# Unread matmuls in two gaps of TensorE: in the first chunk of the linear attention and in double steps 1 and 2 of the softmax attention

## The chip, the cores and the metric

One core of one Trainium2 chip runs the whole kernel. The metric is the device time of one launch in microseconds (us). TensorE (PE) multiplies matrices into the eight banks of PSUM; VectorE (DVE), ScalarE (ACT) and GpSimd (POOL) work on what it leaves there; SyncE (SP) starts transfers. The engines run at the same time, each in its own order, and wait for one another through semaphores. The profile also gives the clock that TensorE was granted in each stretch: 1.00 is 2.4 GHz, 0.50 is 1.2 GHz.

## The reference

A small language model tower on two sequences of 2048 tokens and 128 features: token embedding plus position, then a linear-looking attention with 8 heads of 16, then a block with a softmax attention of 2 heads of 64 and a dense mixture of 8 experts of width 512.

```python
h = tok(x)                                   # embedding + position
h = h + attn(layernorm(h))                   # 8 heads: scores masked, normed, no softmax
h = h + ffn(layernorm(h))                    # 2 heads softmax attention, then 8 experts

# attn
dots = where(causal_mask, 0.0, q @ k.T * scale)
mu = diagonal(cum_mean(dots)); t = dots - mu
s = diagonal(cum_mean(t * t))
out = where(causal_mask, 0.0, t * rsqrt(s + EPS) * norm_g + norm_b) @ v

# ffn
scores = where(causal, l2norm(q) @ l2norm(k).T * sqrt(dh), min)
y = (softmax(scores) @ v) @ Wo
out = sum_e softmax(y @ gate_W + gate_b)[e] * (gelu(y @ W1[e] + b1[e]) @ W2[e] + b2[e])
```

## The kernel before

The two sequences are worked on side by side. There are three stages, and each engine has its own program, written out by hand; only semaphores order the engines against one another.

**The linear attention** goes through 16 chunks of 128 tokens of each sequence. From chunk 1 on (`step_a`) it needs only running sums of earlier chunks. Chunk 0 has no earlier chunk and is computed directly. For each sequence b, PE makes the masked scores (`dots`), DVE subtracts the mean (line 700, semaphore `attn0`), PE transposes the eight heads (line 1097, semaphore `attnT0_ps`), ACT copies them from banks 3 and 4 to memory (line 466, semaphore `attnT0_sb`) and PE multiplies each head with its values, as sixteen instructions of 128x16 (an fp32 matmul stands as two instructions in the profile, a transpose as one). Before its copy of sequence 0 ACT has eight squares to make (line 460). PE's order there is: transposes of sequence 0, the 128x16 set of sequence 0, transposes of sequence 1, the sums of sequence 1, the 128x16 set of sequence 1, then the transposes of chunk 2's normed rows (`xn_T`, line 1025) and chunk 1's `step_a`. `xn_T` of chunk 2 waits for DVE, which first takes the state of sequence 1 out of PSUM (line 655) and then norms the rows (line 647).

**The projections** of the softmax attention (`step_b`) follow by chunk. In the first five of its steps PE already issues `NWARM` = 4 matmuls of 128x512 in fp16 into bank 5 whose results nobody reads.

**The softmax attention** runs in 80 double steps (both heads). In step s PE makes the scores of step s (`scores`), row scores whose only use is a row maximum for a later block (`lone_scores` for the first blocks, one head at a time, into bank 3 or 4), and the products with the values of step s - 2 (`values`). Each lone score is reduced by DVE (line 860) and PE may overwrite its bank only after that (semaphore `sm_used`). Steps 0 and 1 also hold the last two chunks' transposes (`unit_T`), and the first lone scores of step 1 wait for the keys' low halves of chunk 14, which DVE makes (line 829). **The experts** fill the rest, from about 490 us on.

All matmuls are recorded under line 1017, the line of the helper `mm`. Bank 1 holds a chunk's queries and keys in the first stage and is free once ACT has read them (`qkT_sb`); bank 5 is free in steps 1 and 2 of the softmax attention.

Of the kernel before, what the change touches and what calls it, by code (L numbers as in the profile page):

```python
# [23 lines left out]
CH = 512  # L24
# [19 lines left out]
def tower(nc, ids, emb_rows, consts, consts16, rows, cols, w_qkv, w_out, w_sm, w_o, w_gate, w12_rows, b2, out):  # L44
    with ExitStack() as ctx:
        def sb(name, shape, dt=F32):
            return ctx.enter_context(nc.sbuf_tensor(name, shape, dt))

        def sem(name):
            return ctx.enter_context(nc.semaphore(name))  # L50


        cst = sb("cst", [P, C_END])
        c16 = sb("c16", [P, K16 * P], F16)
        row = sb("row", [P, R_END])
# [25 lines left out]
        ident = cst[:, C_ID:C_ID + P]  # L81
# [5 lines left out]
        minus16, onehot = c16[:, 0:P], c16[:, P:2 * P]  # L87
# [81 lines left out]
        ps = ctx.enter_context(nc.psum_tensor("ps", [P, 8, 512], F32))  # L169
# [10 lines left out]
        S = {name: sem(name) for name in names.split()}  # L180
# [832 lines left out]
        def _(pe):  # L1013
            t_ = nc.tensor

            def mm(o, l, r, start=True, stop=True):
                return t_.matmul(o, l, r, start=start, stop=stop, skip_group_check=True)  # L1017
# [42 lines left out]
            def sums(c, par, b, first=False, state=True):  # L1060
                pe.wait_ge(S["qkv_sb"], 2 * c + b + 1)
                if not first:
                    pe.wait_ge(S["x_sb"], 2 * c + b - 1)
                mm(ps[:, 5 + b, 0:D].rearrange("p (h e) -> p h e", e=DA), upper, kv[par][:, b, :, DA:2 * DA], stop=first)
                if not first:
                    mm(ps[:, 5 + b, 0:D], last_row, V1[1 - par][:, b], start=False)
                    pe.wait_ge(S["sg_ready"], 2 * c + b - 1)
                    mm(ps[:, 5 + b, D:D + HA * XW], qT[par][:, b], sg[:, b], start=False)
                if not state:
                    return  # L1070
                if not (first and b == 0):
                    pe.wait_ge(S["sgc_ready"], 2 * c + b)
                mm(ps[:, 7, 0:HA * XW], qk[par][:, b, D:], kv[par][:, b].rearrange("p h w -> p (h w)")
                   ).then_inc(S["state_ps"], 1)
# [17 lines left out]
            for b in range(B):  # L1092
                pe.wait_ge(S["attn0"], b + 1)
                if b:
                    pe.wait_ge(S["attnT0_sb"], b)
                for h in range(HA):
                    last = t_.transpose(ps[:, 3 + h // 4, h % 4 * P:(h % 4 + 1) * P], dtm[:, b, h], ident)
                last.then_inc(S["attnT0_ps"], 1)
                if b:
                    sums(0, 0, 1, first=True)  # L1100
                pe.wait_ge(S["attnT0_sb"], b + 1)
                for h in range(HA):
                    at = D + h * XW + DA
                    last = mm(ps[:, 5 + b, at:at + DA], dtm[:, b, h], kv[0][:, b, h, DA:2 * DA], start=False)
                last.then_inc(S["x_ps"], 1)
# [70 lines left out]
            def unit_T(c):  # L1176
                pe.wait_ge(S["qkn_ready"], c + 1)
                if c >= 2:
                    pe.wait_ge(S["lo_ready"], c - 1)
                if c == NT - 1:  # L1180
                    pe.wait_ge(S["vlo_ready"], NT)
                for i in range(4):
                    b = i % 2
                    last = t_.transpose(ps[:, t_bank(c), i * P:(i + 1) * P],
                                        qkn[:, b, i // 2 * P:(i // 2 + 1) * P], ident)
                last.then_inc(S["qkd_ps"], 1)
# [62 lines left out]
            def lone_scores(it, r, kb, w, k, h):  # L1249
                nonlocal guard  # L1250
                c, b = ITEMS[it]
                q, at, g = b * N + c * CH + r * P, b * N + kb * CH, k + h
                half = slice(h * DS, (h + 1) * DS)
                if g < 10:
                    pe.wait_ge(S["lo_ready"], NT - 1)
                else:
                    pe.wait_ge(S["sm_used"], g - 1)
                if it == 2 and (r, kb) == (0, 0):
                    pe.wait_ge(S["hi_ready"], NT)
                last = mm(ps[:, 3 + g % 2, 0:w], qh[half, q:q + P], kh[half, at:at + w], stop=kb < c)  # L1260
                if kb == c:
                    for z in range(2):
                        last = mask(ps[:, 3 + g % 2, w - P:w], z, h, neg_qk)
                last.then_inc(S["sm_ps"], 1)
                guard = S["sm_used"], g + 1
# [33 lines left out]
            def scores(s):  # L1299
                it, kt, r0, diag = STEPS[s]  # L1300
                c, b = ITEMS[it]
                if s == 0:
                    pe.wait_ge(S["hxT_sb"], NT)
                    pe.wait_ge(S["lo_ready"], 4)
                if s < 2:
                    pe.wait_ge(S["qkn_ready"], NT - 1)
                    pe.wait_ge(S["vlo_ready"], NT - 1)
                if s == FIRST[2]:
                    pe.wait_ge(S["lo_ready"], NT)
                if s:  # L1310
                    pe.wait_ge(S["s_used"], 2 * s - 1)
                lo, at = r0 * P, b * N + kt * P
                q0 = b * N + c * CH
                for still, moving in ((kh, qh), (kl, qh), (kh, ql)):
                    for h in range(HS):
                        half = slice(h * DS, (h + 1) * DS)
                        mm(ps[:, (2 * s + h) % 3, lo:], still[half, at:at + P], moving[half, q0 + lo:q0 + CH],
                           start=still is kh and moving is qh, stop=False)
                if diag:
                    for z in range(2):  # L1320
                        for h in range(HS):
                            mask(ps[:, (2 * s + h) % 3, lo:lo + P], z, h, neg_kq)
                if s in FIRST:
                    pe.wait_ge(S["mrow_sb"], it + 1)
                for h in range(HS):
                    half = slice(h * DS, (h + 1) * DS)
                    last = mm(ps[:, (2 * s + h) % 3, lo:], onehot[half], qm[half, it % 2, lo:], start=False)
                last.then_inc(S["s_ps"], 1)
# [54 lines left out]
            for s in range(NSTEP + LAG + 6):  # L1383
                if s < NSTEP:
                    scores(s)
                if s < 2:
                    unit_T(NT - 2 + s)
                lone = [(*part, h) for part in MSLOT.get(s, ()) if part[0] in ALONE for h in range(HS)]
                pairs = [part for part in MSLOT.get(s, ()) if part[0] not in ALONE]
                assert not (lone and pairs)  # L1390
                closing = min(len(pairs), 1) if s >= CLOSE else len(pairs) // 2
                for part in lone[:1]:
                    lone_scores(*part)
                for part in pairs[:len(pairs) - closing]:
                    pair_scores(*part)
                if s in RAT:
                    max_row(RAT[s])
                if LAG <= s < NSTEP + LAG:
                    values(s - LAG, 0)
                for part in lone[1:2]:  # L1400
                    lone_scores(*part)
                if LAG <= s < NSTEP + LAG:
                    values(s - LAG, 1)
                for part in lone[2:]:
                    lone_scores(*part)
                if s < CLOSE:
                    for part in pairs[len(pairs) - closing:]:
                        pair_scores(*part)
                for m in range(LAST):
                    if s - YAT[m] in PE_Y:  # L1410
                        out_part(m, PE_Y.index(s - YAT[m]) + 1)
                if s >= CLOSE:
                    for part in pairs[len(pairs) - closing:]:
                        pair_scores(*part)
# [82 lines left out]
NWARM = 4  # L1497
PR, QR = 6, 6
WLATE = [2, 7, 13]
LAG = 2  # L1500
CLOSE = 36
K16 = 8
PE_Y, ACT_Y, DVE_Y = [1, 2, 3, 7, 8], [1, 2, 4, 7], [3, 5, 9]
ITEMS, STEPS, FIRST, MSLOT, RAT, OAT, YAT = plan()
# [9 lines left out]
def t_bank(c):  # L1514
    return 6 if c == NT - 1 else 3 + c % 2
# [29 lines left out]
def constants():  # L1545
# [16 lines left out]
    c[:, C_POS:C_END] = pe.reshape(NT, P, D).transpose(1, 0, 2).reshape(P, NT * D)  # L1562
    c16 = np.zeros((P, K16, P), np.float16)
    c16[:, 0] = -np.eye(P)
    c16[[0, DS], 1] = 1.0
    for z in range(2):
# [3 lines left out]
        c16[:, 6 + z] = np.where(src[:, None] > i[None, :], NEG, 0.0)  # L1570
    c16 = c16.reshape(P, K16 * P)
    return c, c16
# [40 lines left out]
```

## Time and profile before

| what | value |
|---|---|
| median of 3 runs | 843.1 us (841.3 to 844.11) |
| the profiled execution, its own time | 841.75 us |
| its span, first to last instruction | 839.9 us |
| PE busy | 775.5 us, 92% of the span |
| DVE, ACT, POOL busy | 702.7, 487.1, 336.7 us |
| mean granted clock of TensorE | 0.98 |

The span is what the trace shows; 1.85 us of the execution lie outside it. An engine's busy time is summed over stages with different bounds, so a stretch is read by itself: which engine is waited for there, and at which clock TensorE ran. "PE" rows are matmuls, "PEld" rows the loads of their stationary operands.

### The profile page before, as it was taken

How to read it: one execution, taken by the hardware profiler on the slowest of the kernel's cores; microseconds unless marked ns; L12 is line 12 of the kernel's file. 1: busy time of each engine (PE TensorE's matmuls, PEld its weight loads, DVE VectorE, ACT ScalarE, POOL GpSimd, SP SyncE). 2: the span in 40 equal slices, each digit the busy share in tenths (PEclk: the TensorE clock that was granted, in tenths of full speed). 3: DMA queues.
4: the chain of work that ended last, by engine and by line, in shares of the span. 5: the costliest groups of instructions: out<-in, count | busy, mean ns of one | idle time of the engine just before them, and what ended most of it. 6: DMA issues, size and time to landing. Idle time of an engine off the chain costs nothing.

```text
span 839.9 us, 21024 instructions
## 1 busy us (share of the span) xinstructions
PE 775.5 (92%) x8208; PEld 554.4 (66%) x8208; DVE 702.7 (84%) x1575; ACT 487.1 (58%) x1023; POOL 336.7 (40%) x374
## 2 busy tenths in 40 slices
PE   1699999999888789998989989999999999999997
PEld 1578778877655455554656556777777777777775
DVE  3649989999678676777676989999999999999997
ACT  2435555555388567777888766455555555555553
POOL 6638999877575557666766621000000000000000
PEclk9879999999999899999999999999999999999999
DMA  4100111000000000000000000000000000000000
GB/s 131 57 8 20 39 38 35 17 27 14 1 1 1 26 2 2 3 2 2 2 3 2 3 13 2 5 12 8 8 5 12 5 11 5 12 4 12 2 14 13
DMA packets 9666, 12.09 MB, mean 14 GB/s; under 512 B 1856, under 2 KB 6592, under 8 KB 9568
## 3 DMA queue, kind: packets, MB, share of 16 engines
q1 hardware_dynamic: 8544, 8.65, 3.4%
q0 software_dynamic: 1024, 2.10, 0.9%
q8 instruction: 65, 1.06, 0.5%
q14 instruction: 33, 0.27, 0.1%
HBM read 8.65 MB, written 2.10 MB: 13 GB/s over the span
## 4 chain that ended last, share of the span: by engine, by line
PE 77%; DVE 11%; issue 4%; ACT 4%; POOL 3%; DMA 1%; another core or an unknown queue 0%; DVEq 0%; ACTq 0%
PE ps L1017 75%; DVE mx L865 2%; POOL ss L345 2%; DVE room L971 1%; DVE room L973 1%; ACT room L591 1%; DVE qkn L819 1%; DVE ss L804 1%; DMA h_all<-emb_rows,idx 1%; DVE och L940 1%; DVE mx L860 1%; ACT room L582 1%; PE ps L1025 1%; PE ps L1045 0%; POOL sm L282 0%
## 5 line engine op out<-in xcount | busy, mean ns | idle before, releaser
L604 ACT ACTIVATE cst<-ps,col 128x512 f32<-128x512 f32 x256 | 175.7, 688 | 161.1 <-PE ps L1017 160.3
L1017 PEld LDWEIGHTS ps<-arena,sq 128*128 128x128 f16 x3072 | 192.1, 98 | 61.8 <-DVE sq L1001 4.3
L1017 PE MATMUL ps<-arena,sq 128*128 128x128 f16 x3072 | 213.0, 219 | 0.5 <-DVE sq L1001 0.5
L1017 PE MATMUL ps<-y,arena 128*128 128x512 f16 x768 | 208.7, 382 | 1.3 <-DVE och L940 1.3
L1001 DVE TENSOR_TENSOR sq<-cst,sq 128x512 f16<-128x512 f32 x256 | 176.7, 690 | 4.4
L383 POOL TENSOR_TENSOR room<-room 128x512 f16<-128x512 f32 (+3 forms) x122 | 123.3, 1029 | 76.7 <-ACT room L591 76.0
L996 DVE CAST sq<-cst 128x512 f16<-128x512 f32 x256 | 109.2, 426 | 10.5 <-ACT cst L604 3.1
L582 ACT ACTIVATE room<-ps 128x512 f32<-128x512 f32 (+3 forms) x160 | 76.8, 534 | 45.6 <-PE ps L1017 45.3
L865 DVE TENSOR_REDUCE mx<-ps 128x2 f32<-128x1024 f32 (+2 forms) x64 | 70.2, 1096 | 35.1 <-PE ps L1017 34.9
L1017 PEld LDWEIGHTS ps<-y,arena 128*128 128x128 f16 x768 | 65.1, 98 | 34.3 <-issue 4.1
L1017 PEld LDWEIGHTS ps<-v,room 128*128 128x128 f16 x1632 | 56.1, 98 | 33.1 <-issue 14.6
L989 DVE SCALAR_TENSOR_TENSOR h_all<-ps,gs,h_all 128x128 f32<-128x128 f32 x256 | 77.1, 343 | 0.9 <-PE ps L1017 0.9
L1017 PE MATMUL ps<-v,room 128*128 128x65 f16 (+1 forms) x1632 | 66.8, 195 | 8.5 <-DVE och L940 5.1
L591 ACT CAST room<-room 128x512 f16<-128x512 f32 (+3 forms) x142 | 72.5, 562 | 0.0
L1017 PEld LDWEIGHTS ps<-room,y 128*128 128x128 f32 x512 | 64.1, 201 | 6.4 <-ACT y L466 5.4
L1017 PE MATMUL ps<-room,y 128*128 128x34 f32 (+1 forms) x512 | 63.3, 279 | 4.6 <-ACT y L466 4.6
L268 POOL TENSOR_TENSOR sm<-sm,mhalf 128x16 f32<-128x16 f32 x15 | 43.6, 2908 | 25.5 <-DVE sm L746 22.1
L1017 PE MATMUL ps<-kh,qh 64*128 64x512 f16 (+3 forms) x160 | 34.0, 363 | 12.1 <-DVE mx L865 8.6
L751 DVE TENSOR_TENSOR y<-ps,cst 128x1024 f32<-128x1024 f32 x30 | 36.3, 1210 | 7.6 <-PE ps L1017 7.6
L973 DVE TENSOR_TENSOR room<-room 128x512 f16<-128x512 f32 (+3 forms) x38 | 36.4, 957 | 3.8 <-ACT room L591 3.1
L1017 PE MATMUL ps<-y,room 64*128 64x512 f32 x128 | 36.8, 655 | 0.0
L239 POOL DMA_INDIRECT h_all<-emb_rows,idx x32 | 31.6, 988 | 10.1 <-issue 7.9
(164 smaller groups left out, 1177.1 us busy)
## 6 DMA issues: line engine op xcount, KB each, us to landing
sq<-w_rows SPq DMA_DIRECT2D x13, 256.0 KB
out<-h_all SPq DMA_DIRECT2D x32, 64.0 KB, 1.6
cst<-consts SPq DMA_DIRECT2D x1, 896.0 KB
h_all<-emb_rows,idx POOLq DMA_INDIRECT x32, 5.3
hxT<-w_rows SPq DMA_DIRECT2D x2, 256.0 KB
cst<-consts SPq DMA_DIRECT2D x1, 398.0 KB, 4.0
c<-consts SPq DMA_DIRECT2D x1, 256.0 KB, 5.5
x<-w_rows SPq DMA_DIRECT2D x1, 256.0 KB
```

The source lines that it names most:

```text
L268: g.tensor_tensor(sm[:, 4], sm[:, 3], mhalf[:].rearrange("p (b h) -> p b h", b=B), ALU.pow).then_inc(S["r_ready"], 1)
L383: g.tensor_tensor(plo[:, i % PR, lo:], p32[:, i % QR, lo:], phi[:, i % PR, lo:], ALU.subtract).then_inc(S["plo_pool"], 1)
L582: a.activation(p32[:, i % QR, lo:], ps[:, i % 3, lo:], ACT.Exp).then_inc(S["s_used"], 1)
L591: a.copy(phi[:, i % PR, lo:], p32[:, i % QR, lo:]).then_inc(S["p_ready"], 1)
L604: a.activation(hid[:, f], ps[:, HBANK[f], :], ACT.Gelu_apprx_tanh, bias=col[:, K_B1 + k:K_B1 + k + 1], scale=1.0 / WS).then_inc(S["hid_rea ...
L751: v.tensor_tensor(dtm[:, b], ps[:, 3:5, :].rearrange("p z (h j) -> p (z h) j", j=P), upper.unsqueeze(1).to_broadcast([P, HA, P]), ALU.mult ...
L865: v.tensor_reduce(mx[:, it % 2, r, kb], ps[:, 3:5, 0:w], AX, ALU.max).then_inc(S["sm_used"], 1)
L973: v.tensor_tensor(plo[:, i % PR, lo:], p32[:, i % QR, lo:], phi[:, i % PR, lo:], ALU.subtract).then_inc(S["plo_dve"], 1)
L989: v.scalar_tensor_tensor(hr, ps[:, EBANK[n % 2], r * D:(r + 1) * D], gs[:, m, r, n % E:n % E + 1], hr, ALU.mult, ALU.add).then_inc(S["eo_u ...
L996: v.tensor_copy(hhi[:, f], hid[:, f]).then_inc(S["hhi_ready"], 1)
L1001: v.tensor_tensor(hlo[:, f], hid[:, f], hhi[:, f], ALU.subtract).then_inc(S["hlo_even" if f % 2 == 0 else "hlo_odd"], 1)
L1017: return t_.matmul(o, l, r, start=start, stop=stop, skip_group_check=True)
```

## The change

It adds matmuls whose results nobody reads, at three places of PE's program, and nothing else. `ident`, `minus16` and `c16` are constants; `cst[:, 0:CH]` is the first 512 columns of the constants, in fp32, and `c16[:, 0:CH]` is fp16.

```diff
@@ the first chunk, for b in range(B) @@
                 last.then_inc(S["attnT0_ps"], 1)
                 if b:
                     sums(0, 0, 1, first=True)
+                else:
+                    pe.wait_ge(S["qkT_sb"], 2)
+                    for i in range(NWARM):
+                        mm(ps[:, 1, :], ident, cst[:, 0:CH])
                 pe.wait_ge(S["attnT0_sb"], b + 1)
@@ the softmax attention, step s @@
                     scores(s)
                 if s < 2:
                     unit_T(NT - 2 + s)
+                for i in range(WARM_C.get(s, 0)):
+                    mm(ps[:, 5, :], minus16, c16[:, 0:CH])
                 lone = [(*part, h) for part in MSLOT.get(s, ()) if part[0] in ALONE for h in range(HS)]
@@ constants of the plan @@
 CLOSE = 36
+WARM_C = {1: 5, 2: 3}
 K16 = 8
```

The orders of DVE, ACT, POOL and SP are what they were. On PE, in the first chunk, four matmuls now stand between the transposes of sequence 0 (`y` is the memory that holds its scores, `cst` the identity) and the 128x16 set of sequence 0, where before one followed the other:

```order
 L1097 MATMUL ps<-cst,y 128x128 [waits attn0]
 L1097 MATMUL ps<-cst,y 128x128 x7
+L1017 MATMUL ps<-cst 128x512 [waits qkT_sb]
+L1017 MATMUL ps<-cst 128x512 x3
 L1017 MATMUL ps<-room,y 128x16 [waits attnT0_sb]
 L1017 MATMUL ps<-room,y 128x16 x7
```

What stood there, the wait for `attnT0_sb`, now comes after the four; they wait for `qkT_sb` alone, ACT's reading of chunk 1's queries and keys.

On PE, in double step 1, five matmuls now stand between the transposes of the last chunk (`unit_T`, `qkn`) and the first lone scores (`kh,qh`, which wait for `lo_ready`):

```order
 L1017 MATMUL ps<-c 128x128 x4
 L1017 MATMUL ps<-room,c 128x384 x2
-L1184 MATMUL ps<-cst,qkn 128x128 [waits vlo_ready,lo_ready,qkn_ready]
-L1184 MATMUL ps<-cst,qkn 128x128 x3
+L1188 MATMUL ps<-cst,qkn 128x128 [waits vlo_ready,lo_ready,qkn_ready]
+L1188 MATMUL ps<-cst,qkn 128x128 x3
+L1017 MATMUL ps<-c 128x512 x5
 L1017 MATMUL ps<-kh,qh 128x128 [waits lo_ready]
 L1017 MATMUL ps<-c 128x128 x2
```

The transposes' rows stand twice only because their line number moved by four; the five matmuls are what is new, and they carry no wait.

On PE, in double step 2, three stand between the scores of step 2 (their last part is `room,c`) and the first lone score, which waits for `sm_used`:

```order
 L1017 MATMUL ps<-c 128x128 x4
 L1017 MATMUL ps<-room,c 128x256 x2
+L1017 MATMUL ps<-c 128x512 x3
 L1017 MATMUL ps<-kh,qh 128x384 [waits sm_used]
 L1017 MATMUL ps<-c 128x128 x2
```

Again nothing moved but the three.

## Rows read from the trace of the kernel before

**Rows 1.** The profile's page: span, and TensorE's granted clock in 40 slices.

```profile
span 839.9 us, 21024 instructions
...
PEclk9879999999999899999999999999999999999999
```

**Rows 2.** Stretches: from:to, length, then each engine's busy us (instructions), clock, DMA.

```profile
31.75:36.30 4.55, 0.00 (x0) 0.00 (x0) 4.28 (x9) 2.47 (x11) 1.67 (x3) 0.77 0.12 32
36.30:47.00 10.70, 10.69 (x46) 9.72 (x46) 2.10 (x10) 1.79 (x5) 5.66 (x8) 0.50 0.16 51
47.00:51.30 4.30, 4.30 (x12) 2.54 (x12) 1.23 (x1) 0.90 (x3) 0.00 (x0) 0.50 0.00 0
286.83:297.07 10.24, 9.89 (x88) 6.05 (x89) 5.40 (x10) 1.98 (x8) 2.11 (x4) 0.50 0.01 2
```

**Rows 3.** Chain of waits in the first chunk: start us, us, what.

```profile
33.20 1.96 another core or an unknown queue
...
35.25 1.02 ACT y L466
...
36.31 3.59 PE ps L1017 x16
```

**Rows 4.** The same chain in steps 2 to 4 of the softmax attention.

```profile
286.75 3.62 PE ps L1017 x36
...
291.96 5.15 PE ps L1017 x36
```

**Rows 5.** PE in order of time, first chunk: start us, us, engine, line, operation, count.

```profile
30.70 1.04 PE L1097 MATMUL ps<-cst,y 128*128 128x128 f32 x8
36.31 3.59 PE L1017 MATMUL ps<-room,y 128*128 128x16 f32 x16 [4.57 <-ACT y L466]
39.75 1.95 PE L1097 MATMUL ps<-cst,y 128*128 128x128 f32 x8
...
42.85 3.60 PE L1017 MATMUL ps<-room,y 128*128 128x16 f32 x16
...
55.08 1.87 PE L1017 MATMUL ps<-room,y 128*128 128x34 f32 x16
```

**Rows 6.** DVE in order of time, between chunk 0 and chunk 2.

```profile
43.06 0.44 DVE L655 TENSOR_TENSOR room<-ps,cst 128x272 f32<-128x272 f32 x1 [6.93 <-PE ps L1017]
...
45.74 0.60 DVE L647 TENSOR_SCALAR room<-h_all,mv,rs 128x128 f32<-128x128 f32 x2 [1.09 <-POOL rs L253]
```

**Rows 7.** PE in order of time: matmuls of the added kinds elsewhere, at clock 1.00.

```profile
238.45 1.03 PE L1017 MATMUL ps<-c 128*128 128x512 f16 x4
...
306.64 1.12 PE L1017 MATMUL ps<-room,wo 128*128 128x512 f32 x2
```

**Rows 8.** PE in order of time: gaps ahead of the lone scores of steps 1 and 2.

```profile
284.11 0.24 PE L1017 MATMUL ps<-kh,qh 64*128 64x128 f16 x2 [1.50 <-DVE kl L829]
...
286.75 0.46 PE L1017 MATMUL ps<-kh,qh 64*128 64x384 f16 x1 [0.79 <-DVE mx L860]
```

**Rows 9.** DVE in order of time: row maxima from step 2 on, with idle time before.

```profile
287.46 0.56 DVE L860 TENSOR_REDUCE mx<-ps 128x1 f32<-128x384 f32 x1 [0.43 <-PE ps L1017]
288.88 0.56 DVE L860 TENSOR_REDUCE mx<-ps 128x1 f32<-128x384 f32 x1 [0.86 <-PE ps L1017]
290.39 1.29 DVE L860 TENSOR_REDUCE mx<-ps 128x1 f32<-128x512 f32 x2 [0.96 <-PE ps L1017]
...
293.64 0.69 DVE L860 TENSOR_REDUCE mx<-ps 128x1 f32<-128x512 f32 x1 [1.10 <-PE ps L1017]
294.79 1.29 DVE L860 TENSOR_REDUCE mx<-ps 128x1 f32<-128x512 f32 x2 [0.46 <-PE ps L1017]
297.13 3.31 DVE L860 TENSOR_REDUCE mx<-ps 128x1 f32<-128x512 f32 x6 [1.06 <-PE ps L1017]
...
302.15 0.56 DVE L860 TENSOR_REDUCE mx<-ps 128x1 f32<-128x384 f32 x1 [0.21 <-PE ps L1017]
303.00 0.56 DVE L860 TENSOR_REDUCE mx<-ps 128x1 f32<-128x384 f32 x1 [0.29 <-PE ps L1017]
```

## The prediction, made before the changed kernel was run

> **What bounds the kernel now.** I read the page first. PE is busy for 92% of the span, so whatever lengthens or shortens its work in a stretch where it is the one waited for moves the end. The row of its clock [rows 1] shows it at full speed but for a few slices. A closer table of stretches [rows 2] shows two long ones at clock 0.50: from 34.25 us to 51.3 us, of which three rows stand there, and the 10.24 us from 286.83. The row from 31.75 to 36.30 has no matmul and a mean clock of 0.77: the clock fell in it, after some 2.5 us of idle PE, to 0.50. It then stayed there for 15 us, though PE was busy for 10.69 of the next 10.70. What PE did in that time was thin: sets of 128x16, transposes, sums [rows 5]. It came back only after the wide matmuls of chunk 1 (the row 47.00 to 51.30). So a busy PE isn't enough; what it does counts.
>
> The chain of waits then tells whether a slow PE matters there. In the first chunk it runs over ACT's copy and then PE [rows 3], from 36.31 on PE alone. In the softmax attention it runs over PE for 3.62 and 5.15 us of the 10.24 [rows 4]. Both stretches are on the path, and a faster PE shortens them until something else ends last.
>
> **The change, part by part.** Nothing is removed or moved; three groups of matmuls are added, and each has a price and a possible gain.
>
> *First group, price.* Four fp32 matmuls are eight instructions of 128x512. Two of that kind took 1.12 us with the tail of the second [rows 7], so eight take at most 4.5. From the end of the transposes at 31.74 (30.70 + 1.04, rows 5) they end by 36.24, and PE's next work starts at 36.31, waiting for ACT's copy. Price: nothing, as ACT's squares and copy cover it, but with hardly any room at that bound. The wait for `qkT_sb` names what ACT finished before its squares, so nothing waits.
>
> *First group, gain.* The idle time of 4.57 us [rows 5] shrinks to between 0.1 us and about 1, so I expect no fall at 34.25. What follows at full clock: the 128x16 set of sequence 0 takes 3.59 us at 0.50, and a set of sixteen 128x34 at 1.00 takes 1.87, so 1.72 less. The transposes of sequence 1 take 1.95 against 1.04, so 0.91 less. After that come more thin work and, now that PE is faster than ACT and DVE, more waiting; at half clock such work could not lift the clock in 10.7 us [rows 2], so I expect that it can't hold it either. I let the clock fall behind the transposes and leave the rest as it was: 1.72 + 0.91 = 2.6 us. Bounds: below, 0, if the thin work loses the clock at once. Above, the clock holds throughout: 10.69 + 4.30 = 15.0 us of PE work at half clock would be 7.5 at full. Of that some 1.1 goes back to a wait: from DVE's state at 43.06 to the end of its norms at 46.34 pass 3.28 us [rows 6] that PE's clock doesn't shorten. It would start at about 39.7 (half of the 6.75 us since 36.31 saved) and end at 43.0. PE would be there at about 41.9 (the second set ends at 46.40; about 4.5 us of the work before it saved). So 6.4 at most. I take 2.6, nearer to the lower end, for the thinness of what follows.
>
> The Trainium skill, "TensorE: Matmul & The Clock Gate", Part 4, says that transposes do not count as activity for the clock as matmuls do. The row of eight transposes at 39.75, at clock 0.50 from first to last, agrees, though the sets around them would explain it too. By that rule the clock falls before the transposes and the term is 1.72 instead of 2.6.
>
> *Second and third group, price.* Four fp16 matmuls of 128x512 took 1.03 us [rows 7]: about 0.26 each, the last one's tail included, so five take at most 1.3 and three 0.8. The gaps where they go are 1.50 us ahead of 284.11, ended by DVE's `kl`, and 0.79 us ahead of 286.75, ended by a row maximum [rows 8]. They fit at full clock, the three just so. If the clock were at 0.50 there they would take twice as long: about 1.1 and 0.8 us over.
>
> *Second and third group, gain.* Between 282 and 287 PE had these gaps and, between them, matmuls over half the rows of the array; the clock fell at 286.83. With both gaps filled the sparse time is gone, and I expect no fall. Then DVE's row maxima are next. In the slow stretch DVE waited for PE six times: 0.43 + 0.86 + 0.96 + 1.10 + 0.46 + 1.06 = 4.87 us [rows 9]. At full clock, later in the same loop, it still waited 0.21 and 0.29. Six waits of 0.25 leave 1.5, so the stretch shrinks by 4.87 - 1.5 = 3.4 us. Bounds: 0, if the clock falls all the same; 4.9, if no wait is left. I take 3.4, since the loop at full clock is the nearest row. From there everything, POOL and ACT too, is driven by these scores, so the gain passes on to the end.
>
> *Sum.* 2.6 + 3.4 = 6.0 us. Against the profiled execution's own time: 841.75 - 6.0 = 835.7. That execution is 1.35 us under the median, so against the median: 843.1 - 6.0 = **837.1 us**. All times below are against the median.
>
> **The rivals.**
>
> *The first gap buys nothing.* Its matmuls keep the clock for their own length, the clock falls in the thin work right behind, and it comes back with the same wide matmuls of chunk 1. For it: 10.7 us of thin work did not lift the clock [rows 2]. Against it: even a delayed fall leaves some of the first set at full clock. Time: 843.1 - 3.4 = 839.7.
>
> *The first gap buys all.* The clock holds to chunk 1: 843.1 - 6.4 - 3.4 = 833.3. For it: in other thin places the clock holds, such as the sets of 128x34 at 55.08. Against it: those stand between wide matmuls, the first chunk's don't.
>
> *The change does not do what it says in the softmax attention.* The clock falls there at another moment, for instance in the lone scores of steps 3 and 4, whose matmuls use half the rows. Then only the first term is left: 840.5. If both places fail, it is 843.1.
>
> The Trainium skill, "TensorE: Matmul & The Clock Gate", Part 1 ("What's actually happening"), says that the activity monitor runs on by itself and isn't reset when a kernel starts. No single trace can show that. By it, a fall or rise lands elsewhere from run to run, so one execution shows one draw of each place; the falls near 229 and 492 us are such draws too, and stay as they are.
>
> *Slower: the first group stands in the way.* ACT's copy started at 35.25, 2 us after its last square, and the chain puts 1.96 us of this down to an unknown releaser [rows 3]. The copy waits for the transposes' semaphore, and the transposes are drawn as ended at 31.74. If they really end at about 35.2, the eight added instructions begin there. At full clock they end 4.5 us later, at 39.7, which is 3.4 after 36.31 and eats the whole of the other gain: 843.1. At half clock they take up to 9.0 and end at 44.2, 7.9 late, less 3.4: 847.6. It makes the kernel slower from the point at which they end later than 39.7. For it: a wait that no row explains. Against it: the matmuls before and behind those transposes are drawn without a break up to 31.74, at the pitch of full clock.
>
> **How the numbers follow.** A measurement can tell about 0.3% from no change, 2.5 us here.
>
> - Forecast, 837.1 (with the first term between 1.5 and 4, the second between 2.5 and 4.5): 0.48.
> - First gap buys nothing, 839.7: 0.20; in about a quarter of this the gain stays under 2.5 us.
> - First gap buys all, 833.3: 0.10.
> - Softmax attention fails, 840.5: 0.07; about half of this under 2.5 us.
> - Both fail, 843.1: 0.08.
> - In the way: 0.07, of which 0.05 lose more than 2.5 us.
>
> Faster: 0.48 + 0.15 + 0.10 + 0.03 = 0.76. Slower: 0.05. Same: 0.19. The range goes from 834.2, which leaves out most of the case that buys all, to 840.6, which takes in the third case whole and the single failure: about 0.2 lies outside.
>
> **What the changed kernel's profile would show.** Right: eight matmuls `ps<-cst` behind the transposes at about 31.7, ended by 36.3; the 128x16 set of sequence 0 in 1.9 us instead of 3.59; no stretch at clock 0.50 between 283 and 297, and waits of DVE before its row maxima of about 0.25. Wrong: the clock back at 0.50 before 37 (first term), a 0.50 stretch of some length among the lone scores (second term), or ACT's copy, and PE's set behind it, later than 36.3, with the eight drawn ahead of it (in the way). If both stretches are at full clock and the end has not moved by about 6, another engine had taken over and the terms' cover was misread: for the second, DVE without idle time and yet no earlier.

## The result, and the profile after

The changed kernel takes 837.27 us (median, 836.6 to 837.8) where the kernel before takes 842.8 beside it: ratio 0.9942, interval 0.9922 to 0.9962, some 5 us faster. The prediction was 837.1 us. In a second series it took 837.34 against 843.66: 0.9931, interval 0.9915 to 0.9946. The profiled execution took 836.98 us, 4.8 less than the profiled one of before.

The page of the kernel after, its span and its row of the granted clock, for [rows 1]:

```profile
span 835.2 us, 21056 instructions
...
PEclk9999999999999999999999999999999999999999
```

Both dips of [rows 1] are gone at this resolution. Four stretches of after (from:to, length, busy us of PE, PEld, DVE, ACT, POOL, clock, DMA) stand against [rows 2]:

```profile
32.70:36.12 3.42, 3.42 (x12) 2.61 (x11) 3.35 (x10) 2.76 (x18) 1.04 (x2) 0.50 0.14 38
38.95:46.36 7.41, 6.00 (x49) 5.30 (x49) 2.10 (x10) 1.89 (x6) 5.03 (x8) 1.00 0.20 69
46.36:50.40 4.04, 4.04 (x13) 2.02 (x11) 1.23 (x1) 0.79 (x3) 0.00 (x0) 0.58 0.00 0
283.25:296.58 13.33, 12.03 (x165) 7.73 (x165) 10.97 (x23) 7.27 (x20) 6.21 (x9) 1.00 0.01 2
```

The clock is at 0.50 from 32.70 to 36.12: it fell ahead of the added group and came back while the group ran. The first chunk's thin work then runs at 1.00 up to 46.36; the clock falls behind it and is back before 50.40. The softmax stretch has no fall at all.

**The first chunk.** PE of after in order of time (start us, us, engine, line, operation, shape, count), for [rows 5]:

```profile
33.20 1.92 PE L1097 MATMUL ps<-cst,y 128*128 128x128 f32 x8
34.91 4.20 PE L1017 MATMUL ps<-cst 128*128 128x512 f32 x8
38.95 1.85 PE L1017 MATMUL ps<-room,y 128*128 128x16 f32 x16
40.65 1.07 PE L1097 MATMUL ps<-cst,y 128*128 128x128 f32 x8
...
42.88 1.96 PE L1017 MATMUL ps<-room,y 128*128 128x16 f32 x16 [0.47 <-ACT y L466]
...
53.79 1.87 PE L1017 MATMUL ps<-room,y 128*128 128x34 f32 x16
```

ACT of after, the last of its squares and the copy that the set of sequence 0 waits for:

```profile
35.27 0.19 ACT L460 ACTIVATION_READ_ACCUMULATOR sq<-y 128x1 f32 x1
36.14 1.01 ACT L466 COPY y<-ps 128x1024 f32<-128x1024 f32 x1 [0.68 <-PE ps L1097]
```

The set of sequence 0 takes 1.85 instead of 3.59 us, the transposes of sequence 1 1.07 instead of 1.95, the set of sequence 1 1.96 instead of 3.60. But the added group isn't free here: the copy ends at 37.15, and the set begins at 38.95. In before and in a run below the set follows the copy after 0.05 us, so the group costs 1.75 us. The chain of waits (start us, us, what) says the same: from the transposes on it stays on PE, through the group and the set.

```profile
33.41 1.71 PE ps L1097 x8
35.12 5.68 PE ps L1017 x24
```

From the transposes of sequence 0 to chunk 1's 128x34 set pass 20.59 us (33.20 to 53.79) instead of 24.38 (30.70 to 55.08, rows 5): 3.79 less. Of this only 1.29 is seen at 53.79, because the transposes began 2.50 us later than in before. That lateness arose in code that the change doesn't touch, as these rows of PE at the start show, of before and then of after:

```profile
21.16 0.94 PE L1017 MATMUL ps<-wqkv,room 128*128 128x128 f32 x6 [1.19 <-ACT room L421]
22.02 1.99 PE L1017 MATMUL ps<-y,room 64*128 64x512 f32 x8
```

```profile
21.18 1.65 PE L1017 MATMUL ps<-wqkv,room 128*128 128x128 f32 x6 [1.19 <-ACT room L421]
22.76 3.52 PE L1017 MATMUL ps<-y,room 64*128 64x512 f32 x8
```

Up to 21.2 they agree within 0.02 us; then the same matmuls run at full clock in before and at half clock in after, where the clock rose at 25.9 instead of 20.6. It is a draw between executions: of the fourteen profiles of this study eight began the transposes between 29.9 and 31.4 us, six between 32.4 and 33.6, with and without added matmuls. In the eight the clock's first rise came at 18.9 to 20.6 us, in the six at 25.3 to 26.4.

**The softmax attention.** DVE's row maxima of after, idle time in brackets, for [rows 9]:

```profile
286.00 0.56 DVE L860 TENSOR_REDUCE mx<-ps 128x1 f32<-128x384 f32 x1 [0.21 <-PE ps L1017]
286.85 0.56 DVE L860 TENSOR_REDUCE mx<-ps 128x1 f32<-128x384 f32 x1 [0.29 <-PE ps L1017]
287.76 1.29 DVE L860 TENSOR_REDUCE mx<-ps 128x1 f32<-128x512 f32 x2 [0.35 <-PE ps L1017]
...
290.35 1.99 DVE L860 TENSOR_REDUCE mx<-ps 128x1 f32<-128x512 f32 x3 [0.51 <-PE ps L1017]
292.54 3.29 DVE L860 TENSOR_REDUCE mx<-ps 128x1 f32<-128x512 f32 x6 [0.19 <-PE ps L1017]
```

Five waits of 0.19 to 0.51, together 1.55, stand where six made 4.87. And PE around the two groups, for [rows 8]:

```profile
281.21 1.24 PE L1017 MATMUL ps<-c 128*128 128x512 f16 x5
282.88 0.24 PE L1017 MATMUL ps<-kh,qh 64*128 64x128 f16 x2 [0.42 <-DVE kl L829]
...
284.67 0.82 PE L1017 MATMUL ps<-c 128*128 128x512 f16 x3
285.52 0.33 PE L1017 MATMUL ps<-kh,qh 64*128 64x384 f16 x1
```

The five leave 0.42 us of the gap of 1.50, the three fill theirs with 0.82 us. From step 1's first lone row maximum to the next block's maximum over 256 (283.25 to 296.58; in before 284.48 to 301.20) pass 13.33 instead of 16.72 us: 3.39 less. With the 1.29 of the first chunk this makes the 4.7 us between the two spans.

### The profile page after: what moved, and what is told of

It reads as the page before. It is cut to its first block, busy times and chain, and to the rows that moved or that the text cites. A ratio compares the mean times of both kernels' runs of the same rounds, so it can differ in the third digit from the quotient of the medians.

```text
span 835.2 us, 21056 instructions
## 1 busy us (share of the span) xinstructions
PE 775.4 (93%) x8224; PEld 551.6 (66%) x8224; DVE 701.7 (84%) x1575; ACT 486.7 (58%) x1023; POOL 337.4 (40%) x374
## 4 chain that ended last, share of the span: by engine, by line
PE 77%; DVE 11%; issue 5%; ACT 3%; POOL 3%; DMA 1%; DVEq 0%; ACTq 0%; POOLq 0%
PE ps L1017 75%; DVE mx L865 2%; POOL ss L345 2%; DVE room L973 1%; DVE room L971 1%; ACT room L591 1%; DVE qkn L819 1%; DMA h_all<-emb_rows,idx 1%; DVE ss L804 1%; DVE mx L860 1%; ACT room L582 1%; DVE och L940 1%; PE ps L1025 0%; PE ps L1045 0%; POOL sm L282 0%
## 5 line engine op out<-in xcount | busy, mean ns | idle before, releaser
L1017 PEld LDWEIGHTS ps<-room,y 128*128 128x128 f32 x512 | 61.0, 192 | 2.4 <-ACT y L466 0.9
L1017 PE MATMUL ps<-room,y 128*128 128x34 f32 (+1 forms) x512 | 59.9, 272 | 0.5 <-ACT y L466 0.5
L751 DVE TENSOR_TENSOR y<-ps,cst 128x1024 f32<-128x1024 f32 x30 | 36.3, 1211 | 7.1 <-PE ps L1017 7.1
```

The lines of the kernel that those rows point to most:

```text
L751: v.tensor_tensor(dtm[:, b], ps[:, 3:5, :].rearrange("p z (h j) -> p (z h) j", j=P), upper.unsqueeze(1).to_broadcast([P, HA, P]), ALU.mult ...
```

## The experiments

The theory: the first group is worth 2.6 us because thin work runs at full clock, the softmax groups 3.4 because the clock doesn't fall; both need wide matmuls. The rivals: one place gives nothing, or the first group stands in ACT's way. All kernels were compared with the kernel before on the same chip. "128x34" is when chunk 1's set began in the profiled execution (55.08 in before, 53.79 in after); "loop" is the softmax stretch named above (16.72 and 13.33).

| kernel | median us | ratio to before, interval | 128x34 | loop |
|---|---|---|---|---|
| first group alone | 840.10 | 0.9968, 0.9951 to 0.9985 | 53.11 | 14.54 |
| softmax groups alone | 839.94 | 0.9970, 0.9949 to 0.9991 | 54.37 | 13.34 |
| step 1's five alone | 841.94 | 0.9985, 0.9963 to 1.0006 | 55.58 | 16.71 |
| step 2's three alone | 839.41 | 0.9965, 0.9947 to 0.9983 | 54.79 | 13.34 |
| thin instead of wide | 843.58 | 1.0024, 1.0007 to 1.0041 | 56.42 | 16.71 |
| first group of two | 836.35 | 0.9940, 0.9915 to 0.9965 | 52.55 | 13.34 |
| softmax groups doubled, alone | 841.35 | 0.9984, 0.9965 to 1.0004 | 56.54 | 13.89 |
| held through the chunk | 835.06 | 0.9924, 0.9895 to 0.9953 | 50.41 | 13.33 |
| the change again | 837.34 | 0.9931, 0.9915 to 0.9946 | 51.55 | 13.34 |
| two, gathers cut | 836.21 | 0.9909, 0.9896 to 0.9922 | 50.70 | 13.32 |
| held, gathers cut | 835.87 | 0.9916, 0.9887 to 0.9945 | 51.64 | 13.33 |
| before, gathers cut | 840.13 | 0.9970, 0.9951 to 0.9989 | 55.58 | 16.70 |

### Each place alone

First group alone:

```diff
-WARM_C = {1: 5, 2: 3}
+WARM_C = {}
```

> Only the four fp32 matmuls in the first chunk; none in the softmax attention. Theory (both places gain, 2.1 + 3.4 of the measured 5.5 us): 2.1 us faster than before, ratio about 0.9975; in the profile a full clock for the 128x16 set of sequence 0 and the transposes of sequence 1, and the stretch at clock 0.50 near 284 to 297 still there. Rival (the first group starts late, at about 35 us, ends after ACT's copy and eats its own gain): no change, ratio 1.000, and all 5.5 us belong to the softmax attention.

Softmax groups alone:

```diff
-                else:
-                    pe.wait_ge(S["qkT_sb"], 2)
-                    for i in range(NWARM):
-                        mm(ps[:, 1, :], ident, cst[:, 0:CH])
```

> Only the eight fp16 matmuls in double steps 1 and 2; none in the first chunk. Theory: 3.4 us faster, ratio 0.996, no stretch at clock 0.50 between 283 and 297, DVE's waits before its row maxima there 0.2 to 0.5 us each. Rival (first group gains nothing): 5.5 us faster, ratio 0.9935. In the first chunk the profile should show the clock at 0.50 from about 34 to 51 as before, and tell whether ACT's copy again starts some 2 us after its last square.

They gave 2.7 and 2.5 us (0.32% and 0.30% of 842.5), 5.2 together, about what the whole gives: the places add up, and neither is empty. PE of the first group alone:

```profile
30.96 1.80 PE L1097 MATMUL ps<-cst,y 128*128 128x128 f32 x8
32.59 3.60 PE L1017 MATMUL ps<-cst 128*128 128x512 f32 x8
36.61 1.96 PE L1017 MATMUL ps<-room,y 128*128 128x16 f32 x16 [0.42 <-ACT y L466]
38.42 1.09 PE L1097 MATMUL ps<-cst,y 128*128 128x128 f32 x8
...
40.67 3.60 PE L1017 MATMUL ps<-room,y 128*128 128x16 f32 x16
```

The transposes of sequence 0 still ran at half clock (1.80 us). From the group on this execution went as the prediction's first term: the group hidden (the set still waits 0.42 us for ACT), the set of sequence 0 and the transposes at full clock, the second set at half. Without the softmax groups its clock fell twice in the softmax attention, in the loop and again behind it:

```profile
285.09:288.51 3.42, 3.42 (x46) 2.51 (x45) 1.40 (x3) 0.21 (x1) 1.28 (x2) 0.50 0.00 0
308.99:315.82 6.83, 6.24 (x84) 4.50 (x82) 3.52 (x8) 2.08 (x9) 4.62 (x7) 0.50 0.00 0
```

Its loop is 14.54, but that isn't a gain of 2.2 us over before. From DVE's row maximum (line 865) at 304.97 to the one at 320.16 pass 15.19 us; between the same two pass 13.26 in before (309.11 to 322.37) and in after (304.50 to 317.76). The later fall costs 1.93 us. From step 1's first lone row maximum to this point the execution takes 37.64 us, before 37.89, after 34.51.

### Which of the softmax groups

Step 1's five alone, then step 2's three alone, neither with the first group:

```diff
-WARM_C = {1: 5, 2: 3}
+WARM_C = {1: 5}
```

> Only the five matmuls of double step 1. If one filled gap is enough to keep the clock: 3.4 us faster, ratio 0.996. If both gaps have to be filled: the clock still falls near 287, ratio 1.000. In between (it falls in some executions and not in others): ratio 0.998 with a wider spread.

```diff
-WARM_C = {1: 5, 2: 3}
+WARM_C = {2: 3}
```

> Only the three matmuls of double step 2. Same three cases as for step 1 alone: ratio 0.996 if three are enough, 1.000 if both gaps have to be filled, about 0.998 with a wider spread if it depends on the execution. I expect the last for both.

The windows (columns as above) of the five alone, and then of the three alone:

```profile
283.00:288.16 5.16, 3.58 (x41) 2.04 (x36) 2.93 (x9) 4.61 (x13) 4.05 (x4) 1.00 0.01 3
288.16:298.40 10.24, 9.89 (x89) 6.08 (x89) 5.39 (x10) 1.99 (x8) 2.11 (x4) 0.50 0.00 0
```

```profile
284.20:297.54 13.34, 12.04 (x165) 7.74 (x165) 10.98 (x24) 7.28 (x20) 6.22 (x9) 1.00 0.01 2
```

With the five alone the clock falls just as in before, one step later than they stand, and the ratio can't be told from no change. The three alone have the loop of the change and gain 3.0 us by the ratio, though its interval overlaps that of the five. As these two profiles show it, the matmuls must stand close ahead of the sparse stretch, and step 1's are hardly needed.

### Does any work do, or only wide work?

The same three places get matmuls of 16 columns, in more instructions:

```diff
-                    for i in range(NWARM):
-                        mm(ps[:, 1, :], ident, cst[:, 0:CH])
+                    for i in range(16):
+                        mm(ps[:, 1, 0:DA], ident, cst[:, 0:DA])
...
-                    mm(ps[:, 5, :], minus16, c16[:, 0:CH])
+                    mm(ps[:, 5, 0:DA], minus16, c16[:, 0:DA])
...
-WARM_C = {1: 5, 2: 3}
+WARM_C = {1: 20, 2: 12}
```

> The unread matmuls of the change at the same three places and for about the same time, but thin: sixteen fp32 matmuls of 128x16 for the four of 128x512, twenty and twelve fp16 ones of 128x16 for the five and three of 128x512. If what counts is that PE is busy: like the changed kernel, ratio 0.994, no stretch at 0.50 between 283 and 297. If it counts what PE does, as the 10.7 us of thin work at clock 0.50 suggest: ratio 1.000, and the stretch at 0.50 near 284 to 297 is back. I expect the second.

PE in the first chunk and ahead of step 1's first lone scores, and a window of this kernel:

```profile
34.75 4.04 PE L1017 MATMUL ps<-cst 128*128 128x16 f32 x32
38.64 3.27 PE L1017 MATMUL ps<-room,y 128*128 128x16 f32 x16
...
285.44 0.24 PE L1017 MATMUL ps<-kh,qh 64*128 64x128 f16 x2 [1.02 <-DVE kl L829]
```

```profile
288.16:298.40 10.24, 9.89 (x88) 6.06 (x89) 5.42 (x10) 1.97 (x8) 2.11 (x4) 0.50 0.01 2
```

In the first chunk PE was busy through the gap as with the wide group, 4.04 against 4.20 us, and the set behind took 3.27 instead of 1.85. The clock came back during the thin group too, at 35.58, but only up to 38.99, where in after it held to 46.36; with step 1's five alone and no group here at all it was up from 35.57 to 38.98. So as these profiles show it, it counts here what PE computes, not that it is busy. In the softmax attention the 10.24 us at 0.50 are back, but there the run doesn't separate the two: the twenty thin matmuls took 0.65 us and left 1.02 of the gap of 1.50, the twelve took 0.46 and left 0.40 of 0.79. By the ratio the kernel is 2.0 us slower than before (0.6 to 3.5 by its interval). The profile doesn't show where: the loop takes 16.71 us as before, and from the transposes to the 128x34 set pass 23.37 us, in before 24.38.

### How many

Two instead of four in the first gap, softmax groups as in the change:

```diff
-                    for i in range(NWARM):
+                    for i in range(2):
```

> The changed kernel with two instead of four fp32 matmuls in the first chunk (1.7 us at full clock instead of 3.4). If four stand in the way of the 128x16 set after them (in the changed kernel's profile they ended 1.75 us after ACT's copy): up to 1 us faster than the changed kernel, ratio 0.993, and the set starts right behind ACT's copy. If their number is what brings the clock back: slower than the changed kernel by 1 to 2 us, ratio 0.996, the set of sequence 0 back at 3.6 us.

Doubled softmax groups, without the first group:

```diff
-WARM_C = {1: 5, 2: 3}
+WARM_C = {1: 10, 2: 6}
```

> Ten and six fp16 matmuls in double steps 1 and 2, none in the first chunk. The gaps of 1.50 and 0.79 us hold seven and three; the rest, 0.7 and 0.65 us, has no cover. Theory (the price is what does not fit the gap): 1.3 us slower than the eight alone, ratio 0.9985 against 0.997. Rival (PE has room there, since DVE ends last in this loop): no slower than the eight, ratio 0.997.

Two do as well as four (836.35; the intervals of the ratios lie over each other): the clock was up from 32.7 to 42.9 with them, and the set still waited 1.97 us for ACT. Doubled groups show the other end. DVE's first row maxima of step 1 in after, then the same and those of step 2 in that kernel:

```profile
283.25 0.49 DVE L860 TENSOR_REDUCE mx<-ps 128x1 f32<-128x128 f32 x2 [0.43 <-PE ps L1017]
```

```profile
287.22 0.49 DVE L860 TENSOR_REDUCE mx<-ps 128x1 f32<-128x128 f32 x2 [1.02 <-PE ps L1017]
...
290.52 0.56 DVE L860 TENSOR_REDUCE mx<-ps 128x1 f32<-128x384 f32 x1 [1.35 <-PE ps L1017]
```

The waits behind the two groups are 0.43 and 0.21 in after; here they are 0.59 and 1.14 longer. The loops differ by 0.55 us only (13.89 against 13.34), since they begin with the first of these maxima and leave out its own wait. From DVE's line 829 ahead of it to the loop's end pass 15.39 us (285.72 to 301.11), in after 14.23 (282.35 to 296.58): 1.16 more. The ratios say about 1.2 (0.9970 to 0.9984), in intervals that overlap. So the price of "nothing" for five and three holds only up to the gap's size.

### Holding the clock through the first chunk

In the gap nine fp16 matmuls (2.6 us) stand for the four fp32; two more follow the sums of sequence 1, four more stand ahead of chunk 2's `xn_T`:

```diff
+            def warm(n):
+                pe.wait_ge(S["load_s"], 80)
+                for i in range(n):
+                    mm(ps[:, 1, :], minus16, c16[:, 0:CH])
...
                     sums(0, 0, 1, first=True)
+                    warm(2)
                 else:
                     pe.wait_ge(S["qkT_sb"], 2)
-                    for i in range(NWARM):
-                        mm(ps[:, 1, :], ident, cst[:, 0:CH])
+                    warm(9)
...
+            warm(4)
```

> The changed kernel with smaller pieces in the first chunk: nine fp16 matmuls of 128x512 (1.9 us at full clock) for the four fp32 ones, two more in the wait for ACT's second copy, four more in the wait for chunk 2's normed rows. If a clock that is held to chunk 1 gives back the rest of the bound: 1 to 3 us faster than the changed kernel, ratio 0.991 to 0.993, no stretch at 0.50 from 36 to 50. If the clock falls all the same or the pieces stand in the way: ratio 0.994 or more.

A window of this kernel and rows of its PE:

```profile
33.77:50.41 16.64, 14.79 (x89) 9.92 (x87) 8.69 (x26) 3.70 (x9) 8.28 (x11) 1.00 0.12 39
```

```profile
32.74 2.62 PE L1017 MATMUL ps<-c 128*128 128x512 f16 x9
37.10 1.96 PE L1017 MATMUL ps<-room,y 128*128 128x16 f32 x16 [1.74 <-ACT y L466]
```

From 33.77 on the clock stays at 1.00 through the rest of the first chunk, and the 128x34 set begins at 50.41, 4.7 us before that of before. This is the clock that the rival "buys all" counted on, but six more matmuls were needed for it. By the medians it is 2 us faster than the change, in another series and with intervals of the ratios that overlap.

### What ACT's copy waits for

In this profile too the set waits for ACT's copy, and the copy for something that isn't drawn, as in [rows 3]. In nine of the first ten profiles (not where ACT's squares themselves ended later) the copy began 2.8 to 3.2 us after the start of POOL's last gather of embedding rows. So the burst of ten gathers was cut: six stay, four go behind chunk 2's norms. It was put into the version with two matmuls, into the one that holds the clock, and into the kernel before, with the change itself beside them:

```diff
-            gather(6, 16)
+            gather(6, 12)
             coefs(0)
             state_add(0)
             front(2, 0)
+            gather(12, 16)
```

> The changed kernel once more, beside the three below, so that they stand beside it under the same conditions. If the gain of 5.5 us is a property of the kernel and not of the sitting: ratio to the kernel before 0.9925 to 0.996 again, about 837 us. In its profile the start of ACT's first copy of scores (line 466) and the moments at which the clock rises near 20 to 26 us may lie elsewhere; the two terms, 1.9 us for the first 128x16 set and a softmax stretch at full clock, should stand.

> Two wide matmuls in the first gap, the softmax groups as in the change, and POOL's burst of ten gathers cut: six stay, the last four go behind the norms of chunk 2. In all profiles so far ACT's first copy of scores (line 466) starts 2.8 to 3.2 us after the start of POOL's last gather of that burst, even where ACT's squares and PE's transposes ended 2 to 3 us earlier. Theory, the burst holds the copy back: now the last gather starts 5 us earlier, near 28, the copy starts within 1 us of ACT's last square, at about 33.0 to 33.8 instead of 35.0 to 36.1, the 128x16 set follows the two matmuls at about 34.5, and the kernel is 1 to 2 us faster than with the two alone (836.35). Rival, the copy waits for something at a fixed moment or for transposes that end later than drawn: copy still at 35 or later, time unchanged. Second rival, the four late gathers hold back what runs beside them near 46 to 51 us: copy earlier, but no gain in time.

> The version that holds the clock through the whole first chunk (nine, two and four fp16 matmuls, 835.06 us), with the same cut of POOL's burst. Theory, the burst holds the copy back: copy at 33.0 to 33.8, and the 128x16 set as soon as the nine matmuls are through, at about 34.7 to 35.3 instead of 37.1, so 2 us less: about 833. Rival, something else holds it: copy at 35 to 36 and 835 again.

> The kernel before with that cut of POOL's burst alone and no added matmul. Theory, the burst holds the copy back: the copy starts at 33.0 to 33.8, PE idles 2.5 instead of 4.6 us, the 128x16 set of sequence 0 starts near 34.5; 1.5 to 2.5 us faster if the clock falls as before, up to 4 if the shorter idle time keeps it up longer. Rival, something else holds it: no change within 1 us. If the four late gathers cost what the burst cost, a loss of up to 2 us.

The change again, POOL's last gather, ACT's last square and copy:

```profile
32.37 0.96 POOL L239 DMA_INDIRECT h_all<-emb_rows,idx  x1 [0.30 <-issue]
```

```profile
33.04 0.19 ACT L460 ACTIVATION_READ_ACCUMULATOR sq<-y 128x1 f32 x1
35.41 1.01 ACT L466 COPY y<-ps 128x1024 f32<-128x1024 f32 x1 [2.18 <-remote]
```

Two matmuls with the gathers cut, the same (lines are one further), and its PE:

```profile
28.02 0.94 POOL L239 DMA_INDIRECT h_all<-emb_rows,idx  x1 [0.30 <-issue]
```

```profile
33.10 0.19 ACT L461 ACTIVATION_READ_ACCUMULATOR sq<-y 128x1 f32 x1
33.36 1.01 ACT L467 COPY y<-ps 128x1024 f32<-128x1024 f32 x1
```

```profile
31.34 1.92 PE L1098 MATMUL ps<-cst,y 128*128 128x128 f32 x8
33.05 2.01 PE L1018 MATMUL ps<-cst 128*128 128x512 f32 x4
34.90 1.85 PE L1018 MATMUL ps<-room,y 128*128 128x16 f32 x16
```

The copy's wait is gone in all three cut kernels: it begins at 33.36, 35.95 and 34.90, each time within 0.1 us of the last square's end. The later two starts, beyond the expected 33.8, are those of executions with a late start. Only the first is a strong case: in the executions that started late with all gathers in place the copy waited no more than 0.8 us behind its squares. In those that started early it waited 1.5 to 2.8 us, and with the two matmuls, an early start too, moving the gathers took this away. So the burst does hold the copy back. By which path, the runs don't show. In time: the kernel before gains 2.5 us by the ratio, 3.5 by the medians, from the cut alone, and two matmuls with the cut have the lowest ratio of all, 0.9909, where the change on the same chip has 0.9931 (the intervals overlap a little). The version that holds the clock gained nothing from the cut (835.87 against 835.06, in different series), against the 2 us expected: its profiled execution started late, ACT's squares ended at 35.92, and nothing was waiting for the gathers any more. Whether an early start would have paid was not seen.

## Why the prediction was right, point by point

**What bounds it.** Right: in both stretches a clock at 1.00 moved the end, and no other engine took the gain back. A busy PE isn't enough either: the thin group shows it.

**First term, gain.** The size was right, 2.6 predicted, 2.7 in the run with this group alone. The profiles agree on the mean: chunk 1's 128x34 set began at 55.08, 54.37, 54.79, 55.58 and 56.54 in the five profiles without a first group and with the gathers in place (mean 55.3), and at 53.79, 51.55, 53.11 and 52.55 with the change, the change again, the group alone and the group of two (mean 52.8): 2.5 less. Executions that began the transposes early differ by 2.3 (54.75 to 52.40), those that began late too (56.06 to 53.79). The way to it was another one. The prediction had the group keep a clock that would fall at 34.25. In all seven profiles with wide matmuls there the clock fell earlier, between 29.1 and 33.2, and the transposes of sequence 0 ran at half clock; it came back between 32.5 and 36.6, while the group ran (in one case 0.08 us ahead of it), and held to 39.3 or longer. In five of the seven profiles without a wide group it came back at 42.5 or later, in two (step 1's five alone and the thin group) at 35.6, up to 39.0. So the group mostly gave a fallen clock back. The profile of before, on which the prediction rests, is the only one of the fourteen in which the clock outlasted these transposes; why, no run shows. The parts of the term were right only in one of three profiles. "I let the clock fall behind the transposes" came true in the group alone; in the change itself the clock held to 46.36 and to 44.3, so that the second set gained 1.64 too. By the Trainium skill, "TensorE: Matmul & The Clock Gate", Part 4, transposes don't count as activity as matmuls do, and the prediction drew from it that the clock falls ahead of the transposes of sequence 1. It didn't: they took 1.07, 1.07 and 1.09 us, full clock, in all three.

**First group, price.** "Nothing" was the step that failed, with the reserve that the prediction put beside it ("hardly any room"). It took the group at full clock, 4.5 us at most, and its beginning at 31.74. It needed 3.60 to 4.40 us, but the clock had already fallen ahead of it, the transposes took 1.8 to 1.92 us instead of 1.04, and it ended at 39.11, 36.88 and 36.19. Against the copy this costs 1.75 us in the first profile, 0.25 in the second (36.42, the copy's end, to 36.72, the set's beginning, less 0.05) and nothing in the third. In the first profile the price and the longer hold offset each other. Four were too many for this gap; two suffice.

**"In the way".** The rival's mechanism is real, at a smaller size; its premise isn't. It put the copy's unexplained 1.96 us down to transposes that end late. With the gathers cut the copy that needs those transposes began 0.3 us after the group's start (33.05 to 33.36), so they end as drawn. It was the gathers, as far as moving them can show it. The sign that the prediction set for this rival, PE's set later than 36.3 with the eight drawn ahead of it, came in all three profiles (38.95, 36.72, 36.61), but in the last two mostly because the copy itself ended at 36.42 and 36.56.

**Second term.** In the profile exact: 3.4 predicted, 3.39 measured, by six waits of 0.25 that became five of 0.31. In time the runs give 2.5 (both groups alone), 3.0 (the three alone) and 2.2 (ratio of the change to that of the first group alone, 0.9942 to 0.9968): 0.4 to 1.2 less than 3.4. One possible reason is a fall that the prediction didn't count. In three of the fourteen profiles the clock fell again at 309 to 313 us, behind the loop, and cost 1.9, 1.9 and 1.4 us (the first group alone, the doubled groups, the held version with the gathers cut; the stretch of 13.26 us named above took 15.19, 15.12 and 14.70). Two of these are among the nine that have the three matmuls or more in step 2: the groups remove the fall in the loop, not each fall behind it. On the mean of the nine that is 0.4 us. It isn't shown that this is what is missing; the intervals would allow 3.4 too.

**Prices in the softmax attention.** Right: both groups fitted, and nothing waited longer. That the five count for little wasn't foreseen; the prediction treated the two groups as one.

**The other falls.** The ones near 229 and 492 us stayed (227.3 to 230.6 and 486.8 to 490.0 at 0.50 in after), as predicted. They aren't the same in each execution: the first group alone and the held version with the gathers cut have none near 490, and the softmax groups alone have one more, from 213.7 to 217.1. The prediction took from the Trainium skill ("TensorE: Matmul & The Clock Gate", Part 1) that the activity monitor runs on by itself and isn't reset when a kernel starts, and said that no single trace could show it. The two starts above agree with it: the same instructions at the same time, once at full and once at half clock.

## What to carry to other kernels

Unread matmuls paid here where TensorE's sparse stretch lies on the path, where they were wide, stood close ahead of the sparse work and ended before what TensorE waits for: two or three did what four or eight did, thin ones gained nothing, and doubled ones gave back 1.2 us, in intervals that overlap, about what did not fit the gaps. Measure the gap that they must fit at the slow clock, not at the fast one, since the clock may have fallen before they begin. And ask of a wait that no row explains what else ran in that time: in the kernel before, moving four gathers was worth as much as one of the groups. Take several executions before a gain of 0.3% is put down to the clock: it falls at other places from one to the next.

## What was not expected of the hardware

- The clock's first rise came at 20.6 or at 25.9 us with the same work before it, and moved the first chunk's transposes by 2.4 us (means of eight and six profiles). Single profiles of this kernel differ by about that much before the first change of code is reached.
- Sixteen fp32 matmuls of 16 columns kept PE busy for 4.04 us and left the next set at 3.27 us; four of 512 columns kept it busy for 4.20 and left it at 1.85.
- ACT's copy began within 0.1 us of its last square with the gathers cut, but up to 2.84 us later with them in place, 2.8 to 3.2 us after the start of the last gather, though its own data was ready. What in them holds it is open.
